# Moving two recurrence units, half a group norm and the latent transposes between the stages of a fused mixer kernel

## The reference

```python
xn = _layernorm(x)                          # x: 8 x 512 x 256
# s branch: low-rank token mixing, then a recurrence over the tokens, 16 heads of 16 x 16
r, k, v, g = ((xn + dx * lora(lerpx)) @ W.T for each of r, k, v, g)
w = exp(-exp(lora(...)))
def step(st, inp):
    kv = einsum('bhi,bhj->bhij', kt, vt)
    y = einsum('bhi,bhij->bhj', rt, st + u * kv)
    return wt * st + kv, y
s = (silu(g) * _ln(ys, ln_w, ln_b)) @ oW.T  # layer norm over the 16 values of a head
# g branch: latent attention with rotary positions, then 8 experts (2 per token) and a shared one
x1 = xn + _attention(_rmsnorm(xn, w_ln1))
g = silu(x1 + _moe(_rmsnorm(x1, w_ln2)))
out = x + s * g
```

## Time and profile before

| | us |
|---|---|
| median of 3 runs (2270.74 to 2276.09) | 2274.21 |
| the profiled execution | 2276.78 |
| its span, first to last instruction | 2275.0 |
| TensorE busy | 2062.7 (91%) |
| VectorE busy | 1794.2 (79%) |
| ScalarE busy | 974.1 (43%) |
| GpSimd busy | 846.5 (37%) |

### The profile page before, as it was taken

How to read it: one execution, slowest core, us unless ns; L and a number is a source line. 1 busy time by engine, 2 the same in 40 slices (tenths; PEclk the granted TensorE clock), 3 DMA queues, 4 the chain that set the end, 5 groups by cost and what they waited for, 6 DMA issues and landing times.

```text
span 2275.0 us, 37286 instructions
## 1 busy us (share of the span) xinstructions
PE 2062.7 (91%) x11722; PEld 1243.2 (55%) x11723; DVE 1794.2 (79%) x2906; ACT 974.1 (43%) x2556; POOL 846.5 (37%) x666
## 2 busy tenths in 40 slices
PE   7998599997988999998999889998989998899887
PEld 4554599997445445544554455455445544554554
DVE  5997466664697889779897988898798879887985
ACT  3444244442274237334623652373347235612741
POOL 1335200001543364336435542643364346326430
PEclk9999799998999999999999999999999999999998
DMA  6554411113222022211211230222122112302210
GB/s 174 145 158 138 146 54 54 52 55 116 64 57 80 1 65 71 61 37 47 66 47 47 61 86 4 61 66 70 29 56 66 47 47 57 79 15 60 61 48 10
DMA packets 145727, 151.18 MB, mean 66 GB/s; under 512 B 47664, under 2 KB 105648, under 8 KB 145584
## 3 DMA queue, kind: packets, MB, share of 16 engines
q1 hardware_dynamic: 138288, 136.73, 22.0%
q0 software_dynamic: 3072, 8.41, 1.1%
q10 hardware_dynamic: 4224, 4.19, 0.6%
HBM read 121.71 MB, written 27.43 MB: 66 GB/s over the span
## 4 chain that ended last, share of the span: by engine, by line
issue 24%; PE 23%; DVE 18%; POOL 8%; ACT 2%; DMA 0%; POOLq 0%; DVEq 0%; ACTq 0%
PE bank L1375 8%; PE bank L1238 4%; DVE arena L1777 4%; POOL arena L2064 3%; PE bank L1292 3%; DVE arena L1797 3%; DVE arena L1790 3%; PE bank L1255 3%; PE bank L1388 2%; POOL arena L2058 2%; DVE arena L2011 1%; ACT arena L1587 1%; POOL arena L2079 1%; PE bank L1265 1%; DVE arena L1852 1%
## 5 line engine op out<-in xcount | busy, mean ns | idle before, releaser
L2058 POOL TENSOR_TENSOR arena<-arena 128x512 f32<-128x512 f32 x256 | 337.1, 1319 | 567.9 <-DVE arena L1797 491.5
L1375 PE MATMUL bank<-arena 128*128 128x512 f32 (+2 forms) x1312 | 438.6, 489 | 6.8 <-DVE arena L1927 6.8
L1171 PE MATMUL bank<-arena 128*128 128x512 f32 (+2 forms) x768 | 360.5, 614 | 6.8 <-ACT arena L1542 5.4
L1797 DVE TENSOR_TENSOR_SCAN arena<-arena 128x512 f32<-128x512 f32 x256 | 361.9, 1414 | 1.7
L1587 ACT ACTIVATE arena<-bank,arena 128x128 f32<-128x128 f32 (+3 forms) x512 | 266.3, 531 | 194.9 <-DVE arena L1777 193.8
L1375 PEld LDWEIGHTS bank<-arena 128*128 128x128 f32 x1312 | 249.9, 203 | 177.2 <-issue 142.1
L1790 DVE TENSOR_TENSOR arena<-arena 128x512 f32<-128x512 f32 x256 | 249.0, 973 | 40.6 <-DMA arena<-values 36.5
L1238 PE MATMUL bank<-arena 64*128 64x128 f32 (+3 forms) x1024 | 207.5, 481 | 71.4 <-ACT arena L1587 49.7
L1171 PEld LDWEIGHTS bank<-arena 128*128 128x128 f32 (+2 forms) x768 | 139.5, 190 | 198.7 <-issue 171.5
L1777 DVE TENSOR_REDUCE arena<-bank 128x2 f32<-128x256 f32 (+3 forms) x256 | 206.9, 808 | 39.0 <-PE bank L1241 39.0
L1596 ACT ACTIVATE arena<-bank 128x128 f32<-128x128 f32 (+3 forms) x512 | 196.4, 441 | 72.3 <-PE bank L1255 72.3
(11 more groups left out here) (200 smaller groups left out, 2960.8 us busy)
## 6 DMA issues: line engine op xcount, KB each, us to landing
arena<-values SPq DMA_DIRECT2D x256, 256.0 KB, 3.4
arena<-in_L_attn_h SPq DMA_DIRECT2D x16, 512.0 KB, 10.4
arena<-in_W1T SPq DMA_DIRECT2D x8, 1024.0 KB
arena<-in_W2T SPq DMA_DIRECT2D x8, 1024.0 KB
sorted_rows<-arena SPq DMA_DIRECT2D x42, 128.5 KB, 9.9
arena<-sorted_rows SPq DMA_DIRECT2D x40, 128.5 KB, 2.1
arena<-in_b2row SPq DMA_DIRECT2D x40, 128.0 KB, 2.9
gate_rows<-arena SPq DMA_DIRECT2D x39, 128.0 KB, 1.7
```

The costliest lines, as they stand in the source:

```text
L1171: last = nc.tensor.matmul(dst[rows, :], w, x, start=(n == 0), stop=(n == len(pairs) - 1))
L1375: last = nc.tensor.matmul(dst[o], w, x, start=first, stop=last_one)
L1797: nc.vector.tensor_tensor_scan(state[n % STATES][:, 1:T + 1], proj["w"][:, m, :], kv[n % 2], VEC["init"][:, m * HD + j:m * HD + j + 1], AL ...
L2058: nc.gpsimd.tensor_tensor(prods[(n + 2) % PRODS], state[n % STATES][:, 0:T], proj["r"][:, m, :], ALU.mult).then_inc(prod_done, 1)
```

## The change

- `EARLY`, `STEPPED` and `AHEAD` are 2 lower: units 2 and 3 leave `before_attention`, the attention steps do 2 to 19, and two more units are done between the experts (25 to 31 instead of 27 to 31). The reductions of groups 4, 5, 6 and 7 move with them.
- The second half's `read_out` moves to the end of VectorE's experts, and `mean_last` to the end of TensorE's. Centre, square and variance move to the next sequence's `before_attention` (behind the experts for the last sequence).
- The latent transposes go behind q7, with their copy on ScalarE behind the first four exponentials. The banks are the same.
- Behind attention `wo0` and `wo1` get their last group ahead of `wo2` and `wo3`.
- GpSimd's small `head` is cut in two, the first part ahead of the product of unit 30.

```diff
-EARLY = 24
-STEPPED = 22
-AHEAD = 4
+EARLY = 22
+STEPPED = 20
+AHEAD = 2
-QKV = "sp0 sp1 lat q2 q3 q4 q5 q6 q7".split()
+QKV = "sp0 sp1 q2 q3 q4 q5 q6 q7 lat".split()
...
@@ TensorE, before_attention
                 lora_pair(b, "v", "k", th[0])
+                if ended is not None:
+                    var_last(ended)
                 lora_a("d", 4, 1)
@@ TensorE, attention
-                    if i == PSTEPS:
-                        reduce_state(b, STEPPED // 4 - 1)
...
-                for i in range(1, NT):
-                    wo(i, early)
+                wo(1, early)
+                reduce_state(b, STEPPED // 4 - 1)
                 pe.wait_ge(y_out, GROUPS * b + GROUPS)
                 wo(0, [GROUPS - 1])
                 wo(1, [GROUPS - 1]).then_inc(made2, 2)
+                wo(2, early)
+                wo(3, early)
@@ TensorE, experts
-                    if half:
-                        reduce_state(b, STEPPED // 4)
...
-                    if e == 2:
-                        reduce_state(b, EARLY // 4)
-                    elif e == 6:
-                        reduce_state(b, EARLY // 4 + 1)
-                    elif e == ME:
-                        mean_last(b)
+                    for at, g in ((2, 5), (4, 6), (ME, 7)):
+                        if e == at:
+                            reduce_state(b, g)
                     if e:
                         down(e - 1)
-                var_last(b)
+                mean_last(b)
@@ ScalarE, attention
+                    if i == LAG - 1:
+                        act.wait_ge(made, pre.made(b, "lat"))
+                        nc.scalar.activation(lat_tok..., ACT.Copy).then_inc(a_read, 1)
@@ VectorE, before_attention
+                if ended is not None:
+                    center_last(ended)
                 for name in ("v0", "k0", "v1", "k1", "d0", "d1"):
...
                 rotate(2)
-                outer(b, 3)
                 if ended is not None:
                     gate_rows(ended, 1)
                     residual(ended)
-                scan(b, 2)
                 for name in QKV:
-                    if name == "q2":
-                        unit(b, AHEAD - 1)
@@ VectorE, between the experts
-                    if e < 4:
+                    if e < 6:
                         unit(b, EARLY + 4 + e)
-                    elif e == 5:
-                        read_out(b, 1)
+                    elif e == 6:
                         ln_inv(b, 0)
-                    elif e == 6:
+                    elif e == 7:
                         ln_scale(b, 0)
-                    elif e == 7:
-                        center_last(b)
                     elif e == 8:
                         ln_gate(b, 0)
+                        read_out(b, 1)
@@ GpSimd, before_attention
+                if ended is not None:
+                    square_last(ended)
...
-                    elif n == 3:
-                        product(b, 2)
-                        product(b, 3)
```

More of the change, by code:

```diff
@@ L941 @@
         + list(_experts()))
-PRE_BANKS = ([6, 7, 3, 5, 0, 1, 2] + 5 * [3, 5, 6, 7, 0, 1, 2])[:len(PRE)]
+PRE_BANKS = ([6, 7, 3, 5, 0, 1, 2] + 5 * [3, 5, 6, 7, 0, 1, 2])[:len(PRE) - 7] + [0, 1, 2, 3, 5, 6, 7]
 POST_BANKS = (7 * [0, 1, 2, 3, 5, 6, 7])[:len(POST)]
@@ L1137, in sequence @@
                         store_sequence(b - 1)
-                    if n == EARLY + COPIES and not last:
+                    if n == 28 and not last:
                         sp.wait_ge(pv_mm, CHUNKS * b + 2 * CHUNKS)
@@ L1491, in _ @@
             experts(B - 1, True)
+            var_last(B - 1)
             gates(B - 1, 0)
@@ L1576, in before_attention @@
                 nc.scalar.activation(x2, s_in, ACT.Copy).then_inc(x2_kept, 1)
-                act.wait_ge(made, pre.made(b, "lat"))
-                nc.scalar.activation(lat_tok.rearrange("p t c -> p (t c)"), bank[pre.bank("lat")][:, 0:NT * ND], ACT.Copy).then_inc(a_read, 1)
             def attention(b):
@@ L1620, in attention @@
                         exp(2 * i + 1)
+                    if i == LAG - 1:
+                        act.wait_ge(made, pre.made(b, "lat"))
+                        nc.scalar.activation(lat_tok.rearrange("p t c -> p (t c)"), bank[pre.bank("lat")][:, 0:NT * ND],
+                                             ACT.Copy).then_inc(a_read, 1)
                 act.wait_ge(pv_mm, CHUNKS * b + 2 * CHUNKS)
@@ L2021, in _ @@
             experts(B - 1, True)
+            center_last(B - 1)
             ln_inv(B - 1, 1)
@@ L2042, in gather, with head_rstd, head_rms @@
                                          in_offset=bass.IndirectOffsetOnAxis(ap=idx[:, i:i + 1], axis=0)).then_inc(g_loaded, 16)
-            def head(b):
+            def head_rstd(b):
                 g.wait_ge(var_done, b + 1)
                 nc.gpsimd.tensor_tensor(rstd, var_eps, neg_half, ALU.pow).then_inc(rstd_done, 1)
+            def head_rms(b):
                 g.wait_ge(ms_done, b + 1)
@@ L2058, in product, with before_attention @@
                 nc.gpsimd.tensor_tensor(prods[(n + 2) % PRODS], state[n % STATES][:, 0:T], proj["r"][:, m, :], ALU.mult).then_inc(prod_done, 1)
-            def before_attention(b):
+            def before_attention(b, ended):
+                if ended is not None:
+                    square_last(ended)
                 for n, x in enumerate(MIX_ORDER):
@@ L2111, in experts, with square_last @@
                 for n in range(EARLY + 3, UNITS):
+                    if n == UNITS - 2 and not final:
+                        head_rstd(b + 1)
                     product(b, n)
                 if not final:
-                    head(b + 1)
+                    head_rms(b + 1)
+            def square_last(b):
                 g.wait_ge(last_read, 4 * b + 1 + 1)
@@ L2118, in _ @@
             gather(0)
-            head(0)
+            head_rstd(0)
+            head_rms(0)
             g.wait_ge(weights_in, 16 * NW)
-            before_attention(0)
+            before_attention(0, None)
             attention(0)
@@ L2124, in _ @@
                 experts(b, False)
-                before_attention(b + 1)
+                before_attention(b + 1, b)
                 attention(b + 1)
             experts(B - 1, True)
+            square_last(B - 1)
             g.wait_ge(g_loaded, 64 * B)
```

## The result

The changed kernel takes 2302.80 us (median of 4 runs, 2300.46 to 2309.04), the kernel before 2273.16 us (4 runs, 2270.74 to 2276.09). The ratio is 1.0136, with a 95% interval from 1.0115 to 1.0157. The direction is the one forecast, but the loss is 29.6 us instead of 16, and the time lies 2.8 us above the range. The profiled execution took 2302.64 us, its span is 2300.8.

The account below looks back on a forecast made before the run. TensorE was taken as the bound in phase C. Per change of sequence 3.4 + 0.9 - 3.0 + 1.0 = +2.3, seven times +16.1, sequence 0 -3.4, program end +3.5: total +16, 2290 us, range 2272 to 2300.

Parts of the forecast that it names:

- What bounds the kernel: Phase C: TensorE works 194.6 of 212.0 us in a sequence; it gets shorter only where a TensorE wait goes.
- Queries: Ahead of attention: VectorE's query rotations end earlier, so attention's first transpose starts 3.0 us earlier; 3.4 in sequence 0.
- Two units more between the experts: In the experts: VectorE gets 3.6 us more work, without delaying TensorE's experts: 0.
- `read_out`, `mean_last` +3.4 and `var_last` +0.9: Behind the experts: `mean_last` waits for `read_out`, next sequence 3.4 us later; moved `var_last` adds 0.9 where TensorE has no gap.
- The three together without the clock: Per change of sequence: 3.4 for `mean_last`, 0.9 for `var_last`, minus 3.0 at the queries.
- rival two: It cancels: queries gain 4.0, `read_out` 3.0 late, clock costs nothing new; -0.1 per sequence, about 2273 us; chance 0.16.
- Clock: Behind the experts: the 5.7 us gap leaves TensorE's clock low, +1.0 us per sequence beyond today's mean; bounds 0.4 to 3.0.
- Behind attention: Output tiles and reductions: `wo(1)` comes 1.7 us earlier, TensorE's tail is one reduction longer: 0, bounds -1 and +0.7.
- Taking it away gains nothing: End of attention: the reduction at 1332 was free, since the product behind it waited 0.25 us for ScalarE; removal gains nothing.
- End of the program: Second half's norm becomes a chain behind everything; ScalarE's root starts at about 2258.9 instead of 2255.36: +3.5 us.
- The signs that it named: `mean_last` waits 5 to 6 us, query waits under 1, `wo` add 1.7 earlier, second-half norm wait stays, sequences about 214.
- Rival three: Clock stays low long behind the experts: 3.0 instead of 1.0 us in seven sequences, +14, 2304 us; chance 0.14.

Follow-up runs that it names:

- second experiment: Changed kernel with the second half's `read_out` moved from the end of VectorE's experts to behind expert 7's accumulation: 2256.36 us, 0.9941.
- filled pair: Changed kernel and kernel before, each with overwritten matmuls that fit its long waits: 2256.45 us (0.9937) and 2254.48 us (0.9936).
- filled kernel before: Kernel before with fitting overwritten matmuls ahead of both halves' transposes (3 and 4) and ahead of `var_last` (2): 2254.48 us, 0.9936.
- filled one: Changed kernel with fitting overwritten matmuls: 7 ahead of the second half's transposes, 5 ahead of `mean_last`, 1 at step 32: 2256.45 us, 0.9937.
- fourth experiment: Changed kernel with five overwritten 128x512 matmuls ahead of `mean_last` in seven sequences: 2274.47 us, 1.0013.
- kernel with the tail edit alone: Kernel before with only the new order of `wo0` to `wo3` and the reduction of step 32 behind `wo1`: 2284.05 us, 1.0043.

## Why the prediction was right in direction and short in size

- **What bounds the kernel**: right. Where a wait of TensorE was filled by what fits, or its clock kept up, the time fell; in two runs a shorter wait alone changed nothing that can be told (the variance behind the product d, and `ln_scale` behind `head_lerp`).
- **Queries, -3.0 per sequence**: right, a little more. `mean_last` to attention is 60.10 instead of 68.09 us; apart from `mean_last`'s own way there, the part from the first low-rank product to attention fell from 60.92 to 58.28 in a long sequence, with 0.87 for the variance in it: -3.5. The rotations, kept at 13.5 us in the prediction, took 13.0 (1467.44 to 1480.43). The first sine product shrank from 1.25 to 0.69 us, the two others stayed at 1.7. In sequence 0, -5.3 instead of -3.4, of which 1.3 is the clock at the start of the stage: the second experiment, with the same edit, has 55.3 us there against 59.2 before, -3.9.
- **Two units more between the experts, 0**: right. From the router's first product to the end of the last down product it is 57.4 us before and 57.7 after, and the router's products are 0.26 of that.
- **`read_out`, `mean_last` +3.4 and `var_last` +0.9**: right. Beyond the long sequences of before, the first product of the next sequence comes 4.1 us later behind the start of the experts, 1.05 of it because `mean_last` runs at 1.2 GHz (2.07 against 1.02 us), so 3.1 for the wait. TensorE waits 5.14 us, 5.7 were forecast. `var_last` costs 0.9.
- **The three together without the clock**, +1.3 in the prediction: measured by the filled pair, 208.18 against 208.36, -0.2 per sequence. But the filled kernel before still pays for some low clock. Its two shortest sequences last 207.73 us, like the two short ones without fillers, and against these the changed kernel's usual 208.14 is +0.4. Either way rival two (-0.1) was nearer for the waits.
- **Clock, +1.0 (bounds 0.4 to 3.0)**: this is the step that failed. After loses 214.70 - 208.18 = 6.5 us per sequence to it, before 210.78 - 208.36 = 2.4 (3.0 against the 207.73 of its shortest sequences), so the change adds 4.1 (3.5), above the upper bound. By the table, 1.2 of the 4.1 is in the experts (the low clock of the earlier trace rows is now in every sequence, no short one as in the earlier trace rows is left), 1.6 at `mean_last` and behind it, 1.4 at the end of attention. Clock and waits together give +3.9 per sequence instead of +2.3, in seven sequences 11.3 us of the 13.6 between 29.6 and 16. The end of the program adds 2.0, the last attention 1.6, and sequence 0 takes 1.9 off. I had priced the two gaps that existed and none that the change would make.
- **Behind attention, 0 (bounds -1 and +0.7)**: this failed in the same way. "Taking it away gains nothing" was true of the wait, since the values wait for ScalarE in either case. But the reduction kept TensorE at work up to 0.25 us before they came. Without it the end of attention came to +1.4 us per sequence in the changed kernel, all of it clock, since the filled one has 76.41 us there. The removal alone does not do it: the clock fell behind a wait of 1.74 us in the changed kernel and stayed up behind 1.72 in its first sequence, behind 1.75 in the fourth experiment and behind 1.2 in the kernel with the tail edit alone. So it cannot be told from the wait. Why is open.
- **End of the program, +3.5**: 5.5. The root of the second half's norm comes 7.6 us later behind the last attention, 3.0 of it by the low clock in the last experts (60.15 us to `mean_last` against 57.19 in the filled kernel) and 1.5 at `mean_last` and `var_last` (1.53 and 2.08 us instead of 1.02 and 1.13). The stretch behind the root is 2.1 us shorter, by no part of the change: it is 17.5 to 19.6 us in kernels with and without it.
- **The signs that it named**: all that were meant to show it right came, the wait of 5.1 us, 0.7 us at the queries, sequences of about 214 us, the first add of the output tiles earlier (by 1.4 us, not 1.7). None of them looked at the clock behind a wait, which is where the loss was.
- **Rival three** (the low clock stays long behind the experts, 2304 us) gave the time that was measured, at 0.14, but in part by luck. It put the whole of its +3.0 behind the experts, where 1.6 was measured, and kept the +1.3 of the waits, of which +0.4 or less was there. The rule of the Trainium skill (TensorE: Matmul & The Clock Gate, HAM oscillation) that a wait recurring in each iteration makes each start cold, which it tells of waits for DMA, holds for the waits ahead of and behind the experts, where the low clock recurs in all seven sequences. At step 32 the measurements differ from it: the wait of 1.75 us recurs in the fourth experiment too, and attention stays at 76.4 us in all its sequences but the first (76.6). I had the rule and took the other end of the range, "because dense matmuls follow at once". Dense matmuls behind a wait are what pays for it.

## What to carry to other kernels

Where TensorE is the bound, price a wait twice: by its length, and by the matmuls behind it at half the clock. Compare the changed kernel with the old one by its low clock in all sequences, and by how long the same products take there, not only by its waits. Work that seems free because a wait follows it may be what keeps the clock up, so before it is moved, look what else can stand in its place; a useful matmul of 1.02 us there (the mean of the first half) made attention 2.5 us shorter in most sequences. And a wait for another engine does not prove that this engine is the bound: see first whether its work follows TensorE's own.

## What the runs showed of the hardware

- Overwritten matmuls in waits made the kernel before faster by 0.64% and the changed one by 2.0% (1.0136 to 0.9937), though they only add work. They must fit: ones that took 5.35 us in a wait of 3.3 and 8.75 in one of 5.1 cost nearly all of it again (2296 against 2256 us).
- An f32 matmul of 128x512 is two records here and takes 0.87 us at a granted clock of 1.00 (20 records, 8.75 us), one of 128x256 0.45 us (24 records, 5.35 us).
- The same program point with nearly the same wait (1.74 and 1.75 us) had a granted clock of 0.54 over the 3 us behind it in one kernel and of 1.00 in another, and in one kernel it fell in six sequences and not in the first. Sequences of one kernel, equal in their instructions, last 204.9 or 208.2 us with 6.8 or 13.7 us of low clock.
